# Six places for the first key block's attention weights, the weighting issued in one piece, and the first pair's maxima ranked ahead of other batches' layers

## The reference

```
scores = einsum('bhqd,bhkd->bhqk', q, k) / sqrt(16)   # causal, 512 x 512 for each of 32 heads
probs  = softmax(scores)
out    = einsum('bhqk,bhkd->bhqd', probs, v) @ w_out
```

## Time and profile before

| | |
|---|---|
| median of 3 runs | 2340.5 us (2339.69 to 2342.32) |
| the profiled execution's own time | 2339.58 us |
| its span in the trace | 2337.9 us |
| mean granted PE clock | 0.972 of full |
| PE busy | 2211.4 us, 95% |
| DVE busy | 1423.1 us, 61% |
| ACT busy | 1237.7 us, 53% |
| POOL busy | 509.3 us, 22% |

### The profile page before, as it was taken

One profiled execution on the slowest core, in us unless ns is written; L12 is line 12 of the kernel. 1 busy time (PEld: TensorE's weight loads), 2 busy tenths in 40 slices (PEclk: granted clock), 3 DMA queues, 4 the chain that ended last, 5 costly groups with the idle time before them and its releaser, 6 DMA issues.

```text
span 2337.9 us, 35726 instructions
## 1 busy us (share of the span) xinstructions
PE 2211.4 (95%) x12528; PEld 1175.9 (50%) x12528; DVE 1423.1 (61%) x3153; ACT 1237.7 (53%) x2313; POOL 509.3 (22%) x646
## 2 busy tenths in 40 slices
PE   6788798999999999999999999999998999999998
PEld 5565454545455454555555555554543444444443
DVE  7756778867768586687878887878832222221222
ACT  6466597756657475676767675787761101011010
POOL 4422233223313132232323231322220000000000
PEclk8779899999999999999999999999999999999999
DMA  5001233412313132332423243333222000000000
GB/s 183 1 1 38 82 100 109 154 51 82 111 40 121 36 118 66 97 105 70 128 68 110 67 127 106 119 97 102 74 83 71 5 14 0 18 0 5 14 0 18
DMA packets 135777, 163.24 MB, mean 70 GB/s; under 512 B 42272, under 2 KB 97696, under 8 KB 135328
## 3 DMA queue, kind: packets, MB, share of 16 engines
q1 hardware_dynamic: 135600, 160.97, 22.3%
HBM read 94.19 MB, written 53.35 MB: 63 GB/s over the span
## 4 chain that ended last, share of the span: by engine, by line
PE 81%; DVE 6%; ACT 4%; DMA 4%; issue 2%; SPq 1%; POOL 1%; POOLq 0%; ACTq 0%; DVEq 0%
PE ps L1537 16%; PE ps L1435 9%; PE ps L1465 8%; PE ps L1548 8%; PE ps L1420 7%; PE ps L1444 7%; PE ps L1490 5%; PE ps L1390 3%; PE ps L1395 3%; PE ps L1499 2%; PE ps L1522 2%; PE ps L1309 2%; PE ps L1475 2%; PE ps L1401 2%; ACT big L1731 1%
## 5 line engine op out<-in xcount | busy, mean ns | idle before, releaser
L2144 DVE TENSOR_REDUCE peaks<-ps 128x4 f32<-128x512 f32 x960 | 623.3, 681 | 213.7 <-PE ps L1390 114.6
L1731 ACT ACTIVATE big<-ps 128x512 f32<-128x512 f32 x960 | 548.2, 603 | 295.0 <-PE ps L1420 219.9
L1959 POOL TENSOR_SCALAR_AFFINE_SELECT big<-big 128x512 f32<-128x512 f32 x384 | 257.0, 682 | 869.3 <-ACT big L1731 868.0
L1537 PE MATMUL ps<-xt,big 128*128 128x512 f32 x896 | 390.1, 593 | 2.9 <-issue 2.9
L1420 PE MATMUL ps<-big 99*128 99x512 bf16 (+3 forms) x1536 | 337.9, 300 | 12.4 <-DMA big<-scr_shift 4.6
L1537 PEld LDWEIGHTS ps<-xt,big 128*128 128x128 f32 x896 | 168.8, 190 | 209.2 <-issue 208.0
L1840 ACT ACTIVATE t<-ps 128x512 f32<-128x512 f32 x56 | 33.5, 598 | 453.4 <-PE ps L1537 453.4
L1465 PE MATMUL ps<-xt,big 128*128 128x512 f32 x480 | 246.1, 607 | 1.4 <-ACT xt L1746 1.1
L1435 PE MATMUL ps<-big,vs 128*32 128x512 f32 (+3 forms) x3072 | 239.5, 439 | 6.7 <-POOL big L1959 5.6
L1720 ACT ACTIVATE ps<-cbf 128x512 f32<-128x512 bf16 x384 | 230.4, 605 | 19.2 <-DVE peaks L2144 15.4
L2200 DVE SCALAR_TENSOR_TENSOR t<-rest,t 128x512 f32<-128x512 f32 x56 | 38.7, 691 | 280.1 <-PE ps L1537 275.7
(11 more groups left out here) (232 smaller groups left out, 2917.8 us busy)
## 6 DMA issues: line engine op xcount, KB each, us to landing
big<-scr_q SPq DMA_DIRECT2D x96, 384.0 KB, 4.0
scr_q<-big SPq DMA_DIRECT2D x48, 384.0 KB, 2.9
scr_q<-big SPq DMA_DIRECT2D x48, 256.0 KB, 3.0
recb<-scr_sums SPq DMA_DIRECT2D x96, 128.0 KB
big<-scr_k SPq DMA_DIRECT2D x48, 192.0 KB, 3.3
big<-in_ffn_gu SPq DMA_DIRECT2D x14, 512.0 KB, 5.1
scr_q<-big SPq DMA_DIRECT2D x48, 128.0 KB, 2.9
ctxt<-ots SPq DMA_DIRECT2D x192, 32.0 KB, 2.0
```

What stands on the lines that cost most here:

```text
L1537: mm = pe.matmul(bank_of(kind, n, m), wgu[:, m // 2, c, way, m % 2 * P:(m % 2 + 1) * P], xt[:, c, :], start=(c == 0), stop=(c == DC - 1))
L1731: act.activation(probs[:, i * S:(i + 1) * S], bank_of("exp", g, i), ACT.Exp, scale=1.0 / 16 if attn_of(n) == 1 else 0.25).then_inc(made["p ...
L1959: pool.affine_select(block_, block_, [[0, GQ], [1, P]], ALU.is_ge, zero, base=0, channel_multiplier=-1).then_inc(made["cut"], 1)
L2144: dve.tensor_reduce(to, blocks, AX.X, ALU.max, negate=True).then_inc(made["negmax"], 1)
```

## The change

It has four parts. The ring: `probs` grows to 6144 columns. The first key block now has six places of 512 columns, and an even group uses places 0 to 3, an odd one 2 to 5. For an odd group, units 0 and 1 are heads 2 and 3 and go to places 4 and 5, units 2 and 3 are heads 0 and 1. Units 0 and 1 of a group wait for the weighting two groups back, units 2 and 3 for the first key block's part of the one before. The weighting: `weigh(g)` waits for the last cut and issues all 32 records; it still signals after key block 0 and at the end. The plan: the first 22 items of the list of maxima (the 20 of pair 0 and two of pair 1) stand ahead of the layers of batches 1 to 3. The room for the larger `probs` comes from two tiles: the rotation table is loaded to `t2` and squares are written to `cs` instead of `a`; in the planner the second rotation table's turn waits for the last rotation of pass 3.

```
+def place(g, i):
+    return i + 2 if i > 3 else i if g % 2 == 0 else (4, 5, 2, 3)[i]
-def exp_unit(i):
+def exp_unit(g, i):
     if i < 4:
-        return [(0, i, 0)]
+        return [(0, place(g, i) - 2 * (g % 2), 0)]
...
     if kind == "pv":
-        return [("PE", "pv", k, 300 + columns((512, 384 + 256 + 128)[k[1]], 1.68) - 150 * k[1])]
+        return [("PE", "pv", k, 190 + columns(512 + 384 + 256 + 128, 1.68))]
...
     if name == "probs":
-        return [("exp_full", k), ("pv_full", (n - 1, int(k[1] > 3))) if n else ("y_full", ("l", 0, TJ - 1))]
+        return [("exp_full", k), ("pv_full", (n - 1 - int(k[1] < 2), int(k[1] > 3))) if n > int(k[1] < 2) else ("y_full", ("l", 0, TJ - 1))]
     if name == "pv":
-        return ([("cut", (n, 2 * k[1]))]
+        return ([("cut", (n, 2))]
...
     if name == "tabs":
-        return [("load_rope", k)]
+        return [("load_rope", k)] + ([("rope", (NB - 1, CHUNKS[-1]))] if n == 2 else [])
...
+            if name == "pv":
+                ended["pv_full", key + (0,)] = begin + 1050 + late
...
         for cost, item in prepared(0):
             self.put(item)
-        for q in range(1, NB):
-            for item in layers(q) + (four_bit(q) if q == 1 else []):
-                self.put(item)
         maxes = []
...
+        m = 22
+        for item in maxes[:m]:
+            self.put(item)
+        for q in range(1, NB):
+            for item in layers(q) + (four_bit(q) if q == 1 else []):
+                self.put(item)
...
-            for half, last in ((0, UNITS - 1), (1, UNITS - 1)):
-                due.setdefault(g * UNITS + last + LAG, []).append(("pv", g, half))
+            due.setdefault(g * UNITS + UNITS - 1 + LAG, []).append(("pv", g))
...
+        ropet = t2[:].rearrange("p (j w k) -> p j w k", j=TJ, w=2)
-        big1 = sb("big1", [P, 14336], F32)
+        big1 = sb("big1", [P, 15360], F32)
-        probs = big1[:, 7680:12800]
+        probs = big1[:, 7680:13824]
...
-        def probs_of(key):
+        def probs_of(g, key):
-            lo, hi, at = ((0, 2048, 0), (2048, 4096, 0), (4096, 5120, 0), (2048, 4096, 3 * P))[key]
+            first = 1024 * (g % 2)
+            lo, hi, at = ((first, first + 2048, 0), (3072, 5120, 0), (5120, 6144, 0), (3072, 5120, 3 * P))[key]
...
-            def weigh(g, half_):
+            def weigh(g):
                 n = g // 8
-                pe.wait_ge(made["cut"], counted("cut", g, 2 * half_))
+                pe.wait_ge(made["cut"], counted("cut", g, 2))
...
-                for key in (1, 3, 2) if half_ else (0,):
+                for key in (0, 1, 3, 2):
                     for h in range(GQ):
...
-                mm.then_inc(made["pv_full"], 1)
+                    if key in (0, 2):
+                        mm.then_inc(made["pv_full"], 1)
...
-                if g:
-                    act.wait_ge(made["pv_full"], counted("pv_full", g - 1, int(i > 3)))
+                back = g - 1 - int(i < 2)
+                if back >= 0:
+                    act.wait_ge(made["pv_full"], counted("pv_full", back, int(i > 3)))
```

More of the change, by code:

```diff
@@ L592, in signals @@
             return [("vproj_full", k[:1])] if k[1] == TJ - 1 else []
+        if name == "pv":
+            return [("pv_full", k + (0,)), ("pv_full", k + (1,))]
         if name in ("proj", "gate", "up", "gate3", "up3"):
@@ L694, in try_out @@
             late = 260 if engine == "PE" else 100
-            for end in signals(engine, name, key) + ([(name, key)] if name in ("resid", "tab_p") else []):
+            if name == "pv":
+                ended["pv_full", key + (0,)] = begin + 1050 + late
+            for end in signals(engine, name, key)[int(name == "pv"):] + ([(name, key)] if name in ("resid", "tab_p") else []):
                 ended[end] = begin + ns + late + LANDS.get(name, 0) * (engine == "SP")
@@ L1109, in load_rope @@
                     sp.wait_ge(made["tabs_full"], counted("tabs_full", 1))
[L1110 removed]
+                sp.dma_start(ropet, ins[f"attn{A}_rope"]).then_inc(rope_in, 16)
             def load_ffn1():
@@ L1418, in exp_scores @@
                 bank = bank_for("exp", g, i)
-                for key, h, at in exp_unit(i):
+                for key, h, at in exp_unit(g, i):
                     mm = pe.matmul(bank[:, at:at + S - key * P], kt[0:SROWS, p % 3, g % 2, key * P:(key + 1) * P],
@@ L1422, in exp_scores @@
                 mm.then_inc(made["exp_full"], 1)
-            def weigh(g, half_):
+            def weigh(g):
                 n = g // 8
-                pe.wait_ge(made["cut"], counted("cut", g, 2 * half_))
[L1427 to L1432, removed]
-                for key in (1, 3, 2) if half_ else (0,):
+                pe.wait_ge(made["cut"], counted("cut", g, 2))
+                bank = bank_for("pv", g)
+                if g % 8 == 0:
+                    pe.wait_ge(made[values(n)], counted(values(n), n))
+                    if g == 0:
+                        pe.wait_ge(clearing, 2)
+                for key in (0, 1, 3, 2):
                     for h in range(GQ):
-                        mm = pe.matmul(bank_of("pv", g)[32 * h:32 * h + 32, key * P:S], vs[:, n % 2, key, g % 8, :],
-                                       probs_of(key)[:, h], start=(key == 0), stop=(key == 2), skip_group_check=True)
-                mm.then_inc(made["pv_full"], 1)
+                        mm = pe.matmul(bank[32 * h:32 * h + 32, key * P:S], vs[:, n % 2, key, g % 8, :], probs_of(g, key)[:, h],
+                                       start=(key == 0), stop=(key == 2), skip_group_check=True)
+                    if key in (0, 2):
+                        mm.then_inc(made["pv_full"], 1)
             def dense(n, j, c):
@@ L1725, in weights_of @@
                 n = g // 8
-                if g:
-                    act.wait_ge(made["pv_full"], counted("pv_full", g - 1, int(i > 3)))
-                elif i == 0:
+                back = g - 1 - int(i < 2)
+                if back >= 0:
+                    act.wait_ge(made["pv_full"], counted("pv_full", back, int(i > 3)))
+                else:
                     act.wait_ge(made["y_full"], counted("y_full", "l", 0, TJ - 1))
                 act.wait_ge(made["exp_full"], counted("exp_full", g, i))
-                act.activation(probs[:, i * S:(i + 1) * S], bank_of("exp", g, i), ACT.Exp,
+                act.activation(probs[:, place(g, i) * S:(place(g, i) + 1) * S], bank_of("exp", g, i), ACT.Exp,
                                scale=1.0 / 16 if attn_of(n) == 1 else 0.25).then_inc(made["probs"], 1)
@@ L1821, in squares @@
                         act.wait_ge(made["sq"], counted("sq", *((n, j - 1) if j else (n - 1, TJ - 1))))
-                    act.activation(a[:, 0:D], x_rows(n, j), ACT.Square, accum_out=ssq[:, k:k + 1]).then_inc(made["sq"], 1)
+                    act.activation(cs[:, 0, :], x_rows(n, j), ACT.Square, accum_out=ssq[:, k:k + 1]).then_inc(made["sq"], 1)
             def rows3_out(n, c):
@@ L1957, in cut @@
                 pool.wait_ge(made["probs"], counted("probs", g, KEY_ENDS[key]))
-                block_ = probs_of(key)[:, :, 0:P]
+                block_ = probs_of(g, key)[:, :, 0:P]
                 pool.affine_select(block_, block_, [[0, GQ], [1, P]], ALU.is_ge, zero, base=0, channel_multiplier=-1
```

9 lines of the change are left out of this document (2 added, 7 removed).

## The result

The changed kernel took 2362.9 us (median of five, 2356.8 to 2366.3), the one before 2342.3 us in the same series. The ratio is 1.009, 95% interval 1.0075 to 1.0105: 21 us slower, where I forecast 2325 us and gave "slower" 0.18. The profiled execution took 2362.9 us with a span of 2361.2 us, 23.3 us more than the span before.

A forecast was written before the change was run, and what follows sets the result against it. PE was taken to bound three quarters of the span, chains through several engines the part before 293 us. -10.7 + 2 - 7 = -15.7 us gave 2325 us for the median; eight in ten: 2311 to 2344 us.

The forecast's parts named there:

- slower: Whole kernel: the outcome of a time above what measurement tells from no change (about 4.7 us); chance 0.18.
- The weighting in one piece: PE's 55 parted weightings: each costs 0.24 us more than a whole one, so joining them gives -10.7 us.
- Its new wait: 28 groups outside the middle: whole piece waits for the last cut, 0.07 us each, +2 us; nothing in the middle.
- late pieces: Rival, ACT-heavy stretches: PE and ACT stand before the whole piece, 28 groups lose 25 us, 2350 us in all; chance 0.14.
- The ring: ACT's waits for the weighting: units 0 and 1 lose theirs; valued at 0, its help already taken in the wait's price.
- The front: Ahead of the first exp unit: maxima ranked first bring it 14 us sooner, from 293 to about 279 us; -7 us.
- the front backfires: Rival, front: blocked projections and batches 2 and 3's layers holding banks longer make it +8 us, 2340 us; chance 0.15.
- What costs nothing: Rotation table in `t2`, later place of its turn on PE, 12 squares in `cs`: all priced at nothing.
- the order undoes it: Rival, all of PE's order: new ranks redeal it and draw out other products, 2334 us or no gain; chance 0.15.

The follow-up runs named there:

- e12_ring_quarters: Kernel before with ring of six, late turn of the second rotation table and POOL's bias additions in quarters; weighting in two halves, old plan: 0.9927, 2323.5 us.
- e13_whole_quarters: Kernel before with ring, late turn of the second rotation table, weighting in one piece and POOL's bias additions in quarters; old plan: 0.9999.
- e5_piece: Kernel before with the weighting in one piece alone, ring of four and old plan: 1.0167.
- e2_nofront: Changed kernel without the plan's change, so ring, whole piece and late turn of the second rotation table: 1.0020.
- e9_ring: Kernel before with ring of six and late turn of the second rotation table; weighting in two halves, old plan: 0.9946.
- e16_whole_middle: Kernel before with ring, late turn and POOL's bias additions in quarters, weighting whole in passes 1 to 8 only, halves elsewhere: 0.9932.
- e1_front: Kernel before with the plan's change alone, the first 22 maxima ahead of the layers of batches 1 to 3: 1.0026.
- e17_rank_behind_batch1: Kernel before with ring, late turn, quartered bias additions, two halves; 22 maxima behind batch 1's layers and 4-bit product, ahead of batches 2 and 3's layers: 0.9941.
- e14_front_open: Kernel before with the 22 maxima ahead, but PE may look as far ahead from them as from the first item behind the layers: 1.0028.
- e4_tabs_late: Kernel before with one planner line changed: the second rotation table's turn waits for the last rotation of pass 3: 0.9961.
- e3_tabs_early: Changed kernel with the second rotation table's turn back where the planner had it: 1.0142.
- e6_no_bias_adds: Changed kernel, same orders on every engine, POOL's four bias additions cut to 8 of 512 columns, most biases left out: 1.0020.
- e10_quarters: Changed kernel with each of POOL's bias additions in four pieces of 128 columns, nothing left out: 1.0020.

## Why the prediction was wrong, step by step

To tell idle time from slow clock and from work, I summed PE from each record's start to the next one's; half of the busy time at 1.2 GHz counts as lost to the clock. Before: 120.5 us idle, 48.8 us lost to the lower clock, 2168.6 us of work at the upper one. Changed kernel: 140.8, 59.6, 2160.8 us. So the change saved 7.8 us of work and lost 20.3 us to idle time and 10.8 us to the clock, 23.3 us in sum. These are one execution each, and such sums are not sharp: the work up to the first exp unit comes out as 186 us in e12_ring_quarters and as 192 in e13_whole_quarters, whose orders are the same so far.

**The weighting in one piece, -10.7 us: too large by about a third.** Over the whole trace PE's work fell by 7.8 us. In groups 24 to 71, 24 weightings were parted before and none after, for which 24 x 0.24 = 5.8 us were forecast; PE's work there fell by 4.1 us, 0.7 us a pass instead of 1.0. The weightings fell from 113.4 to 110.1 us, 0.14 us for each parted one, as forecast. The product ahead of a piece is drawn out by 0.09 us in both traces, also as forecast, and the maxima fell by 2.1 us with it. What was not forecast is that the exp products rose by 2.1 us and the output product by 0.9 us; the rest is spread over other products. For the exp products the records say why: 23 of them now stand before idle time instead of 10, and such a one counts with its whole 0.3 us instead of the 0.14 us to the next start. The estimate from the drain in the Trainium skill, "TensorE: Matmul & The Clock Gate", section "Single matmul latency", 0.35 us for each parted weighting, was further off than the row.

**Its new wait, +2 us: this is the step that failed.** Term and wait together were forecast at -8.7 us. Measured, the whole piece costs 39 us without ring and late turn (e5_piece) and 17 us with both, with POOL's additions whole (e2_nofront against e9_ring) as with quarters (e13_whole_quarters against e12_ring_quarters). I looked for the price at the wait for the cut, which indeed stays small: 3.2 us in the changed kernel, and 7.1 us in e13_whole_quarters beside 6.4 in e12_ring_quarters. It is paid elsewhere, in the passes where ACT is busy for 74 to 85% of the time (e16_whole_middle). My reading of the waits is that ACT or PE comes late to the next thing in a fixed order, a mask before a D unit, a shift, and the clock falls with it; no run holds one of these waits fixed. That is the rival "late pieces" with its place and its size (25 us less 8 from the middle, of which the middle gave nothing that can be told), and I gave it 0.14. Its evidence against, PE's short waits for cuts in the kernel before, was no evidence: in two halves PE had the first half to do there.

**The ring, 0.** Beside two halves it is not told from nothing (0.9946 against 0.9961, 0.9927 against 0.9945, the same small sign twice). Beside the whole piece ring and late turn together take off 34 us, of which the late turn accounts for 9 to 12. The rest, more than 20 us, is the ring's: it is what makes the whole piece bearable; I had named that and not priced it.

**The front, -7 us: the second step that failed.** The rank brought the first exp unit 14 us forward, as forecast (though the first maximum, which I held to be fixed, moved too: 244.2 to 239.1 us in e1_front), and its worth had the wrong sign: +6, +16, +10 and +5 us in four pairs of kernels. Of the 16, which is the pair that ends in the changed kernel, some 11 came through POOL's long additions. The rival "the front backfires" was right, with +8 us for this term where I put -7. What carries it is the delay of batch 1 (e17_rank_behind_batch1), not LOOK (e14_front_open). As I read it, an earlier start of the exp units leaves PE the same work, and takes from it the one other thing that it could do while chains of the front run.

**What costs nothing.** The late turn of the second rotation table was no free edit: it frees one of eight PSUM banks from the front to 590 us, and is worth 9 and 12 us (e4_tabs_late, e3_tabs_early). I had looked at the table's DMA and its products, not at the bank that stands between the turn on PE and ACT's copy, which `order_of` shows. That it is the bank, and not the new order that comes with the line, is argued: the worth is alike on two kernels, but no run frees a bank in another way. (The squares are 16 instructions, not 12; nothing hangs on that.)

**What no step had.** The alignment of DVE's split with POOL's bias additions: without it 16 us of the 21 go (e6_no_bias_adds, e10_quarters). Kernels of the same family lose 4 to 5 us to it even in the old plan (e4_tabs_late, e9_ring, e2_nofront, each against itself with quarters), so some 12 us are what the change added; the kernel before was not run with quarters. That new orders move stalls about I had as "the order undoes it", without a place or a price. The trace of before showed it already, a split of 1.8 us beside POOL's additions at 1159 us. The Trainium skill states the rule in "SBUF — State Buffer", section "Who interferes with whom": a DVE instruction in a two-port mode, which a cast can enter, contends with GpSimd, and one with two SBUF inputs contends with a GpSimd instruction that reads SBUF; the later of the two blocks fully; a reduction never contends on trn2. The rows agree in all three: the casts 0.78 and 1.18 us, the subtractions 1.21 and 1.20 us, the reduction 0.28 us as ever.

The parts don't add. -9 (late turn), some -4 (ring, not told from 0), +17 (whole piece), +16 (rank, with the port's stalls in it) make +20, which is the chain from e4_tabs_late over e9_ring and e2_nofront to the changed kernel and so matches by construction; on the kernel before the whole piece costs 39 us and the rank 6. What stays open is by which single waits the whole piece loses its 17 us: they are many and under 4 us each.

## What to carry to other kernels

When a kernel's orders are fixed ahead, a piece that waits for its last input must be judged by what its parts were filling, and in the stretches where the second engine is near its limit, not at its own wait. An edit that looks like bookkeeping should be read for the buffers it holds or frees. Before an order is blamed, look for small VectorE instructions that take several times their usual length, and at what GpSimd runs beside them: cutting that in quarters gave 4 to 5 us on three kernels and 16 on another. Compare each edit with its own partner: against the kernel before, the rank seemed to bring the first exp unit 26 us forward, of which 14 were its own.

## What the hardware showed unexpectedly

A DVE instruction of 32 columns takes 0.18 us alone, and up to 1.2 us beside a 512-column addition on POOL (1.27 us); four in a row take 4.4 us, one for each addition, though each began 0.04 us or less after the last had ended. With additions of 128 columns (0.45 us, one every 0.41 us) they take 0.36 to 0.39 us. Beside POOL's cuts (0.65 us) the casts and subtractions of the split take up to 0.65 us as well. After each of the four turn's waits of 2.7 us PE's granted clock was at 1.2 GHz for 3.4 us; work that takes 3.4 us at that level takes 1.7 us at the upper one, so such a wait cost more than half as much again as its length. In the kernel before, two waits of 1.9 us (901 and 1400 us) were followed by the same 3.4 us, and one of 2.8 us (1532 us) was not.
